# Two of eight experts: gates from one exponential of the second maximum, shares made on GpSimd, the last two halvings on VectorE, fewer filler matmuls

## The chip, the core and the metric

The kernel runs on one core of a Trainium2 chip. The metric is the device time of one execution in microseconds (us), median over runs; lower is better. Engine names in rows: PE is TensorE (matmuls), PEld its weight loads, DVE VectorE, ACT ScalarE, POOL GpSimd, SP SyncE. Everything is fp32, and on PE each matmul of the source shows as two instructions.

## What is computed

Four blocks follow one another on x (8 x 32 x 16 x 16), each a spatial mixer and a channel mixer with residuals. The channel mixer of the first and of the third block is the part that the change touches, a mixture of two experts out of eight for each of 2048 tokens:

```python
def _L0_ffn_ref(x, router_w, router_b, expert_w, expert_b):
    router_probs = jax.nn.softmax(x @ router_w + router_b, axis=-1)
    top_p, top_i = jax.lax.top_k(router_probs, K)            # K = 2 of E = 8
    top_p = top_p / jnp.sum(top_p, axis=-1, keepdims=True)
    expert_out = jnp.einsum('bnd,edc->bnec', x, expert_w) + expert_b
    gathered = jnp.take_along_axis(expert_out, top_i[..., None], axis=2)
    return jnp.einsum('bnk,bnkc->bnc', top_p, gathered)
```

With the maximum subtracted, the best logit is 0 and the second is d <= 0. The two shares are then 1 / (1 + exp(d)) and exp(d) / (1 + exp(d)).

## The kernel before

It is a hand-ordered program: each engine has one function with its instructions in program order, and engines wait for one another on named semaphores. Nothing is scheduled by a tool. The mixture of experts stands in each engine's `top2(turn)`; turn 0 lies at about 33.9 to 47.9 us of the profiled execution, turn 1 at 337.7 to 351.7 us. Tokens lie as 128 partitions x 16 tiles, so the logits LG, the masks S1 and S2, and the gates GW are 128 x 128 (16 tiles x 8 experts); a value per token is 128 x 16.

- VectorE (L762 to L779) makes the gates in a chain of sixteen small instructions, nearly each waiting for the one before. It takes the maximum (L762), subtracts it (L763, LG), finds the first maximum's place with ties broken by the tile `keys` (L765 to L767, S1), masks it (L768), takes the second maximum (L769) and finds its place in the same way (L770 to L773, S2), adds both masks (L774), multiplies by the exponentials EX of all logits (L776), sums (L777), inverts (L778) and scales (L779, GW).
- VectorE then multiplies the eight slots s of expert outputs by their gates (L788, 128 x 512 each, into PR); slots 0 to 3 come from SBUF (EXB), slots 4 to 7 from PSUM banks.
- GpSimd halves the products: L387 adds, for each of slots 0 to 6, the last four experts to the first four (semaphore `halved`). VectorE does slot 7 (L793, `last_halved`).
- ScalarE copies slot outputs 0 to 3 out of PSUM (L471, `keep(s)`, semaphore `expert_kept`) and, between `keep(0)` and `keep(1)`, makes EX from all logits (L475, waits `gate_ready`, which L763 gives).
- TensorE computes experts for slots 0 to 3, adds the residual (L1105), computes experts for slots 4 to 7 in banks that `keep` has emptied (L1203; its slot 4 + k waits for `expert_kept` of slot k), runs `keep_warm(FILL_GATES)`, transposes the gates (L1216), adds the expert biases (L1219), and then sums four experts of two slots into the output, four times (L1228, `pair` 0 to 3, eight instructions each). Ahead of each pair stand `FILL_PAIR` = 2 filler matmuls (L1101, results unused, two instructions each). Pair p waits for halving 2p + 2, pair 3 for halving 7 and `last_halved`. After pairs 1 and 3 `mixed_done` releases the sums of the next norm on VectorE (L708).

Of the kernel before, what the change touches and what calls it, by code (L numbers as in the profile page):

```python
# [18 lines left out]
E8 = 8  # L19
# [27 lines left out]
FILL_LAST = 1  # L47
FILL_TAIL = 16
FILL_KEYS = (0, 3)
FILL_GATES, FILL_PAIR = 4, 2  # L50
FILL, FILL_EC = (13, 18, 12, 6, 5, 9, 12, 8), 2
FILL_HOP, FILL_PROB, FILL_DRAIN = 2, 8, 3
GROUPS3 = 8
# [70 lines left out]
def metaformer(nc, x_in, cst_in, wa_in, wb_in, wc_in, wd_in, out):  # L124
# [3 lines left out]
    with ExitStack() as ctx:  # L128
# [7 lines left out]
        def view(t, col, dims, p0=0, n=P):  # L136

            if isinstance(t, tuple):
                t, first = t
                col = first + col  # L140
            if isinstance(t, Bank):
                t, col = psum, t.at + col
            w = t.shape[1]
            return bass.AP(t, p0 * w + col, [[w, n]] + [list(d) for d in dims])
# [77 lines left out]
        def cv(name, n, c=0, p0=0, np_=P):  # L222
# [23 lines left out]
            sem(n) for n in ("att_ready", "att_turned", "attc_ready", "u_done"))  # L246
        routed, gate_ready, ex_ready, expert_done, expert_kept, weighed = (
            sem(n) for n in ("routed", "gate_ready", "ex_ready", "expert_done", "expert_kept", "weighed"))
        halved, last_halved, mixed_done = sem("halved"), sem("last_halved"), sem("mixed_done")
        pa_set, h_turned, ht_ready = sem("pa_set"), sem("h_turned"), sem("ht_ready")  # L250
        gw_ready, gw_turned, gwt_ready = (sem(n) for n in ("gw_ready", "gw_turned", "gwt_ready"))
# [81 lines left out]
        def _(pool):  # L333
# [47 lines left out]

            def top2(turn):

                for s in range(NT // 2 - 1):
                    pool.wait_ge(weighed, turn * 8 + s + 1)
                    first, last = (view(PR, s * 512 + o, [[256, 2], [1, 128]]) for o in (0, 128))
                    pool.tensor_tensor(first, first, last, ALU.add).then_inc(halved, 1)  # L387
# [27 lines left out]
        def _(act):  # L415
# [52 lines left out]
            def top2(turn):  # L468
                def keep(s):
                    act.wait_ge(expert_done, turn * 8 + s + 1)  # L470
                    act.activation(view(EXB, s * 512, [[1, 512]]), bank[2 + s][:, :], ACT.Copy).then_inc(expert_kept, 1)  # L471

                keep(0)
                act.wait_ge(gate_ready, turn + 1)
                act.activation(EX[:, :], LG[:, :], ACT.Exp).then_inc(ex_ready, 1)  # L475
                for s in range(1, B4):
                    keep(s)
                act.wait_ge(gw_turned, turn + 1)
                act.activation(GT[:, 0:P], bank[1][:, 0:P], ACT.Copy).then_inc(gwt_ready, 1)
# [203 lines left out]
        def _(dve):  # L683
            links = [0]

            def link(ins):

                links[0] += 1
                ins.then_inc(dve_chain, 1)
                dve.wait_ge(dve_chain, links[0])  # L690
# [64 lines left out]
            def top2(turn):  # L755
# [10 lines left out]
                link(dve.tensor_reduce(s16[:, :], by_e(KEY), AX.X, ALU.max))  # L766
                link(dve.tensor_tensor(by_e(S1), by_e(KEY), one(s16), ALU.is_equal))  # L767
                link(dve.scalar_tensor_tensor(by_e(KEY), by_e(S1), -BIG, by_e(LG), ALU.mult, ALU.add))  # L768
                link(dve.tensor_reduce(s16[:, :], by_e(KEY), AX.X, ALU.max))  # L769
                link(dve.tensor_tensor(by_e(S2), by_e(KEY), one(s16), ALU.is_equal))  # L770
                link(dve.tensor_tensor(by_e(KEY), by_e(S2), keys, ALU.mult))
                link(dve.tensor_reduce(s16[:, :], by_e(KEY), AX.X, ALU.max))
                link(dve.tensor_tensor(by_e(S2), by_e(KEY), one(s16), ALU.is_equal))  # L773
                link(dve.tensor_tensor(by_e(S1), by_e(S1), by_e(S2), ALU.add))  # L774
                dve.wait_ge(ex_ready, turn + 1)
                link(dve.tensor_tensor(by_e(GW), by_e(S1), by_e(EX), ALU.mult))  # L776
                link(dve.tensor_reduce(s16[:, :], by_e(GW), AX.X, ALU.add))  # L777
                link(dve.reciprocal(mean[:, :], s16[:, :]))  # L778
                dve.tensor_tensor(by_e(GW), by_e(GW), one(mean), ALU.mult).then_inc(gw_ready, 1)  # L779
                dve.wait_ge(gw_ready, turn + 1)  # L780
                for s in range(NT // 2):
                    if s < B4:
# [2 lines left out]
                    else:  # L785
# [2 lines left out]
                    dve.tensor_tensor(view(PR, s * 512, [[256, 2], [C, E8], [1, C]]), outputs,  # L788
                                      view(GW, (s // 4 * 8 + s % 4) * E8, [[4 * E8, 2], [1, E8], [0, C]]),
                                      ALU.mult).then_inc(weighed, 1)  # L790
                dve.wait_ge(weighed, turn * 8 + 8)
                first, last = (view(PR, 7 * 512 + o, [[256, 2], [1, 128]]) for o in (0, 128))
                dve.tensor_tensor(first, first, last, ALU.add).then_inc(last_halved, 1)  # L793

            def expert_choice(turn, w, at):
                dve.wait_ge(ec_logits, turn + 1)
# [295 lines left out]
        def _(pe):  # L1092
# [93 lines left out]
            def top2(turn, w, at, nx):  # L1186
# [32 lines left out]
                    pe.matmul(moe_out[bh][0][:, 0:NPIX], GT[:, 0:P], w_(w, at["eb"] + bh * NPIX, NPIX), start=False, stop=False,  # L1219
                              skip_group_check=True)  # L1220
                for pair in range(4):
                    keep_warm(bank[0], FILL_PAIR)
                    bh, at_col = pair // 2, pair % 2 * 2 * C
                    pe.wait_ge(halved, turn * 7 + min(2 * pair + 2, 7))
                    if pair == 3:
                        pe.wait_ge(last_halved, turn + 1)
                    for e in range(E8 // 2):
                        ins = pe.matmul(view(moe_out[bh][0], at_col, [[P, 2], [C, 2], [1, C]]), ident,  # L1228
                                        view(PR, pair * 1024 + e * C, [[256, 2], [512, 2], [1, C]]), start=False,
                                        stop=(e == E8 // 2 - 1), skip_group_check=True)  # L1230
                    if pair % 2:
                        ins.then_inc(mixed_done, 1)
# [541 lines left out]
```

## Time and profile before

| | |
|---|---|
| median of three runs | 430.16 us (429.26 to 431.37) |
| the profiled execution: its own time, its span | 431.09 us, 429.3 us |
| PE busy (matmuls, ends modelled) | 385.1 us, 90% |
| DVE / ACT / POOL busy | 337.2 / 289.7 / 167.0 us |
| mean granted TensorE clock | 0.980 of full |
| L387 POOL | 14 instructions, 12.5 us |

A busy share says little here: in each stage another engine ends last. The time from the first to the last instruction (span) is 1.8 us less than the execution's own time. The views below are read at turn 1; turn 0 repeats them.

### The profile page before, as it was taken

The numbers are of one execution on the slowest core, as the hardware profiler recorded it, in microseconds if no ns is written. First come the engines' busy times: TensorE is split into PE (matmuls) and PEld (weight loads), VectorE is DVE, ScalarE is ACT, GpSimd is POOL, SyncE is SP. The second block draws the span as 40 slices with busy tenths as digits, with TensorE's granted clock in tenths as the row PEclk, the third lists the DMA queues.
The fourth block names the chain that finished last, engine by engine and source line by source line (L and its number), as shares of the span: only waits on it lengthen the run. The fifth ranks groups of instructions, "written<-read, shape, count | busy, mean of one in ns | idle before, by whom it ended". The sixth has DMA issues, their size and how long they took to land.

```text
span 429.3 us, 9890 instructions
## 1 busy us (share of the span) xinstructions
PE 385.1 (90%) x4018; PEld 261.6 (61%) x4018; DVE 337.2 (79%) x659; ACT 289.7 (67%) x513; POOL 167.0 (39%) x138
## 2 busy tenths in 40 slices
PE   5689999899899978989999888899999998898897
PEld 5467932223247746767678566667679686555575
DVE  3779697999971685999997677999996776999541
ACT  4755296998936486997751668987821537989471
POOL 4002300000000167799996466999993050000000
PEclk9898999999999998999999989999999899999999
DMA  8300040000024000000000000000000000000000
GB/s 294 129 3 2 2 94 2 2 2 0 2 94 175 2 2 2 2 2 2 2 2 0 2 2 2 2 2 2 2 2 2 0 2 1 2 2 2 2 2 26
DMA packets 1629, 9.29 MB, mean 22 GB/s; under 512 B 208, under 2 KB 976, under 8 KB 1104
## 3 DMA queue, kind: packets, MB, share of 16 engines
q1 hardware_dynamic: 1440, 8.59, 5.7%
q8 instruction: 32, 0.52, 0.5%
q14 instruction: 13, 0.11, 0.1%
q10 hardware_dynamic: 144, 0.07, 0.1%
HBM read 7.40 MB, written 0.26 MB: 18 GB/s over the span
## 4 chain that ended last, share of the span: by engine, by line
PE 40%; DVE 26%; ACT 16%; POOL 11%; issue 6%; DMA 1%; DVEq 0%; SPq 0%; ACTq 0%; POOLq 0%
PE bank L1431 7%; PE bank L1101 6%; PE bank L1353 4%; ACT RINGS L654 4%; POOL wb L371 4%; DVE RINGS L859 3%; DVE RINGS L850 3%; PE bank L1414 3%; PE bank L1575 2%; ACT RINGS L582 2%; PE bank L1555 2%; POOL RINGS L387 2%; POOL PRD L371 2%; PE bank L1342 2%; DVE PRD L953 2%
## 5 line engine op out<-in xcount | busy, mean ns | idle before, releaser
L1431 PE MATMUL bank<-VB,RINGS 64*128 64x144 f32 x1152 | 96.3, 304 | 8.9 <-DVE PRD L953 4.7
L1431 PEld LDWEIGHTS bank<-VB,RINGS 64*128 64x128 f32 x1152 | 77.7, 190 | 32.4 <-issue 15.3
L1101 PE MATMUL bank<-cst 128*128 128x128 f32 x450 | 63.1, 284 | 0.0
L1101 PEld LDWEIGHTS bank<-cst 128*128 128x128 f32 x450 | 56.3, 195 | 5.1 <-issue 2.7
L582 ACT ACTIVATE RINGS<-bank,cst 128x768 f32<-128x768 f32 x48 | 42.5, 886 | 22.1 <-PE bank L1414 22.1
L354 POOL TENSOR_TENSOR HY<-OM,cst 128x324 f32<-128x324 f32 x16 | 12.6, 816 | 113.0 <-DVE LXA L906 113.0
L953 DVE TENSOR_TENSOR wb<-bank,HY 128x864 f32<-128x864 f32 x48 | 50.4, 1049 | 5.4 <-PE bank L1431 5.4
L953 DVE TENSOR_TENSOR PRD<-bank,HY 128x864 f32<-128x864 f32 x48 | 50.2, 1050 | 5.5 <-PE bank L1431 5.5
L585 ACT ACTIVATE RINGS<-RINGS,cst 128x768 f32<-128x768 f32 x48 | 44.9, 936 | 1.6
L523 ACT ACTIVATE RINGS<-PRD,wb 128x2048 f32<-128x2048 f32 (+1 forms) x21 | 39.5, 1920 | 4.5 <-PE bank L1353 3.5
L1353 PE MATMUL bank<-RINGS,cst 128*32 128x512 f32 x336 | 39.7, 594 | 2.4 <-DVE RINGS L859 2.0
L1414 PE MATMUL bank<-RINGS,cst 32*128 32x256 f32 x288 | 35.0, 436 | 5.4 <-ACT RINGS L582 5.3
L371 POOL TENSOR_TENSOR wb<-wb 128x864 f32<-128x864 f32 x16 | 32.5, 2039 | 9.6 <-DVE wb L953 9.6
L371 POOL TENSOR_TENSOR PRD<-PRD 128x864 f32<-128x864 f32 x16 | 32.5, 2031 | 7.9 <-DVE PRD L953 7.9
L387 POOL TENSOR_TENSOR RINGS<-RINGS 128x256 f32<-128x256 f32 x14 | 12.5, 930 | 52.0 <-DVE RINGS L788 52.0
L654 ACT ACTIVATE RINGS<-RINGS,nm 128x256 f32<-128x256 f32 x64 | 31.5, 496 | 1.3 <-DVE nm L1056 1.3
L1353 PEld LDWEIGHTS bank<-RINGS,cst 128*32 128x32 f32 x336 | 10.3, 110 | 28.6 <-issue 18.2
L427 ACT ACTIVATE SQ<-XN 128x256 f32<-128x256 f32 x16 | 6.0, 417 | 31.2 <-DVE XN L713 31.2
L1575 PE MATMUL bank<-cst,RINGS 128*128 128x128 f32 x128 | 20.8, 286 | 4.9 <-ACT RINGS L654 4.4
L1056 DVE CUSTOM_DVE_ANT_0 RINGS<-bank,wd 128x256 f32<-128x256 f32 x64 | 22.7, 421 | 2.8 <-PE bank L1555 2.8
L380 POOL TENSOR_TENSOR PRD<-PRD 128x432 f32<-128x432 f32 (+1 forms) x16 | 24.8, 1575 | 0.0
L1414 PEld LDWEIGHTS bank<-RINGS,cst 32*128 32x128 f32 x288 | 15.5, 188 | 14.0 <-issue 9.5
(277 smaller groups left out, 713.8 us busy)
## 6 DMA issues: line engine op xcount, KB each, us to landing
wd<-in_wd SPq DMA_DIRECT2D x1, 2793.0 KB, 9.9
wb<-in_wb SPq DMA_DIRECT2D x1, 2112.0 KB, 10.3
wc<-in_wc SPq DMA_DIRECT2D x1, 1027.0 KB, 12.3
cst<-in_cst SPq DMA_DIRECT2D x1, 766.0 KB, 5.7
PRD<-PRD SPq DMA_DIRECT2D x1, 324.0 KB, 3.4
PRD<-PRD SPq DMA_DIRECT2D x1, 323.9 KB, 4.7
PRD<-PRD SPq DMA_DIRECT2D x1, 323.8 KB, 5.5
XC<-in_x SPq DMA_DIRECT2D x2, 128.0 KB, 2.4
```

The costliest lines, as they stand in the source:

```text
L371: pool.tensor_tensor(second, second, first, ALU.add).then_inc(paired, 1)
L380: pool.tensor_tensor(second, second, third, ALU.add).then_inc(paired, 1)
L523: return act.activation(out, x, ACT.Abs, scale=-1.0, bias=view(wb, WB["lw"] + 9 * g + tap, [[1, 1]]))
L582: act.activation(view(HX, hx, [[NPIX, 3], [1, NPIX]]), view(bank[4], 0, [[512, 3], [1, NPIX]]), ACT.Abs, bias=cv("mx", 1)).then_inc(abs_do ...
L585: act.activation(view(HX, hx, [[1, 3 * NPIX]]), view(HX, hx, [[1, 3 * NPIX]]), ACT.Relu, scale=-1.0, bias=cv("one", 1)).then_inc(hat_ready, 1)
L654: ins = act.activation(view(SM3, at, [[1, 256]]), view(SM3, at, [[1, 256]]), ACT.Exp, scale=-1.0, bias=nm[:, u:u + 1], accum_out=rs[:, u:u ...
L953: dve.tensor_tensor(view(prd(i, half), t * TRIO, [[3 * COLS, GP], [6 * NR, CG], [1, 6 * NR]]), view(bank[q % 2 * 2], 0, [[512, GP], [6 * N ...
L1101: pe.matmul(bk[:, 0:P], ident, ident, start=True, stop=True)
L1353: ins = pe.matmul(bank[2][32 * j:32 * j + 32, :], cv(rep, 32, 28 - 4 * g), two_images(slot, j), start=(n == 0), stop=(n == len(PE_JOBS) - ...
L1414: pe.matmul(bank[4 + quad][:, 0:NPIX], cv("select", P, t * P, 32 * quad, 32), view(LXT, i % 2 * NPIX, [[1, NPIX]], 32 * quad, 32), start=T ...
L1431: ins = pe.matmul(view(bank[q % 2 * 2 + gp], k3 * NR, [[3 * NR, 2 * CG], [1, NR]]), view(HX, b % 2 * HXN + (3 * t + k3) * NPIX + half * P, ...
L1575: ins = pe.transpose(turned3_bank[s % 3][:, (2 * kt + j) * P:(2 * kt + j + 1) * P], view(SM3, s % 6 * 512 + (2 * j + kt) * P, [[1, P]]), i ...
```

## The change

It makes the gates in another way, spreads them over three engines, moves one halving per turn, and leaves out three filler matmuls per turn. On VectorE the second maximum goes to `var` and is announced (`second_ready`). ScalarE no longer takes the exponential of all logits: it waits for `second_ready`, takes the exponential of the second maximum (128 x 16), waits for its own result, adds 1 to it (`Identity` with bias), and VectorE inverts the sum while it goes on finding the second mask. GpSimd multiplies the exponential by the inverse (tile `sd`) and the first mask by the inverse (S1). VectorE multiplies the second mask by `sd` and adds S1.

```diff
@@ -47,7 +47,7 @@
 FILL_LAST = 1
 FILL_TAIL = 16
 FILL_KEYS = (0, 3)
-FILL_GATES, FILL_PAIR = 4, 2
+FILL_GATES, FILL_PAIR, ON_POOL = 4, (2, 2, 1, 0), 6
 FILL, FILL_EC = (13, 18, 12, 6, 5, 9, 12, 8), 2
 FILL_HOP, FILL_PROB, FILL_DRAIN = 2, 8, 3
 GROUPS3 = 8
...
@@ -381,7 +382,11 @@
 
             def top2(turn):
 
-                for s in range(NT // 2 - 1):
+                by_e = view(S1, 0, [[E8, NT], [1, E8]])
+                pool.wait_ge(ratio_ready, turn + 1)
+                pool.tensor_tensor(sd[:, :], EX[:, 0:NT], mean[:, :], ALU.mult).then_inc(shares_ready, 1)
+                pool.tensor_tensor(by_e, by_e, view(mean, 0, [[1, NT], [0, E8]]), ALU.mult).then_inc(shares_ready, 1)
+                for s in range(ON_POOL):
                     pool.wait_ge(weighed, turn * 8 + s + 1)
                     first, last = (view(PR, s * 512 + o, [[256, 2], [1, 128]]) for o in (0, 128))
                     pool.tensor_tensor(first, first, last, ALU.add).then_inc(halved, 1)
@@ -471,8 +476,10 @@
                     act.activation(view(EXB, s * 512, [[1, 512]]), bank[2 + s][:, :], ACT.Copy).then_inc(expert_kept, 1)
 
                 keep(0)
-                act.wait_ge(gate_ready, turn + 1)
-                act.activation(EX[:, :], LG[:, :], ACT.Exp).then_inc(ex_ready, 1)
+                act.wait_ge(second_ready, turn + 1)
+                act.activation(EX[:, 0:NT], var[:, :], ACT.Exp).then_inc(ex_ready, 1)
+                act.wait_ge(ex_ready, 2 * turn + 1)
+                act.activation(EX[:, NT:2 * NT], EX[:, 0:NT], ACT.Identity, bias=cv("one", 1)).then_inc(ex_ready, 1)
                 for s in range(1, B4):
                     keep(s)
                 act.wait_ge(gw_turned, turn + 1)
@@ -766,17 +773,18 @@
                 link(dve.tensor_reduce(s16[:, :], by_e(KEY), AX.X, ALU.max))
                 link(dve.tensor_tensor(by_e(S1), by_e(KEY), one(s16), ALU.is_equal))
                 link(dve.scalar_tensor_tensor(by_e(KEY), by_e(S1), -BIG, by_e(LG), ALU.mult, ALU.add))
+                dve.tensor_reduce(var[:, :], by_e(KEY), AX.X, ALU.max).then_inc(second_ready, 1)
+                dve.wait_ge(second_ready, turn + 1)
+                link(dve.tensor_tensor(by_e(S2), by_e(KEY), one(var), ALU.is_equal))
+                link(dve.tensor_tensor(by_e(KEY), by_e(S2), keys, ALU.mult))
+                dve.wait_ge(ex_ready, 2 * turn + 2)
+                dve.reciprocal(mean[:, :], EX[:, NT:2 * NT]).then_inc(ratio_ready, 1)
                 link(dve.tensor_reduce(s16[:, :], by_e(KEY), AX.X, ALU.max))
                 link(dve.tensor_tensor(by_e(S2), by_e(KEY), one(s16), ALU.is_equal))
-                link(dve.tensor_tensor(by_e(KEY), by_e(S2), keys, ALU.mult))
-                link(dve.tensor_reduce(s16[:, :], by_e(KEY), AX.X, ALU.max))
-                link(dve.tensor_tensor(by_e(S2), by_e(KEY), one(s16), ALU.is_equal))
-                link(dve.tensor_tensor(by_e(S1), by_e(S1), by_e(S2), ALU.add))
-                dve.wait_ge(ex_ready, turn + 1)
-                link(dve.tensor_tensor(by_e(GW), by_e(S1), by_e(EX), ALU.mult))
-                link(dve.tensor_reduce(s16[:, :], by_e(GW), AX.X, ALU.add))
-                link(dve.reciprocal(mean[:, :], s16[:, :]))
-                dve.tensor_tensor(by_e(GW), by_e(GW), one(mean), ALU.mult).then_inc(gw_ready, 1)
+                dve.wait_ge(shares_ready, 2 * turn + 1)
+                link(dve.tensor_tensor(by_e(GW), by_e(S2), one(sd), ALU.mult))
+                dve.wait_ge(shares_ready, 2 * turn + 2)
+                dve.tensor_tensor(by_e(GW), by_e(GW), by_e(S1), ALU.add).then_inc(gw_ready, 1)
                 dve.wait_ge(gw_ready, turn + 1)
                 for s in range(NT // 2):
                     if s < B4:
@@ -788,9 +796,10 @@
                     dve.tensor_tensor(view(PR, s * 512, [[256, 2], [C, E8], [1, C]]), outputs,
                                       view(GW, (s // 4 * 8 + s % 4) * E8, [[4 * E8, 2], [1, E8], [0, C]]),
                                       ALU.mult).then_inc(weighed, 1)
-                dve.wait_ge(weighed, turn * 8 + 8)
-                first, last = (view(PR, 7 * 512 + o, [[256, 2], [1, 128]]) for o in (0, 128))
-                dve.tensor_tensor(first, first, last, ALU.add).then_inc(last_halved, 1)
+                for s in range(ON_POOL, NT // 2):
+                    dve.wait_ge(weighed, turn * 8 + s + 1)
+                    first, last = (view(PR, s * 512 + o, [[256, 2], [1, 128]]) for o in (0, 128))
+                    dve.tensor_tensor(first, first, last, ALU.add).then_inc(last_halved, 1)
 
             def expert_choice(turn, w, at):
                 dve.wait_ge(ec_logits, turn + 1)
@@ -1219,11 +1228,12 @@
                     pe.matmul(moe_out[bh][0][:, 0:NPIX], GT[:, 0:P], w_(w, at["eb"] + bh * NPIX, NPIX), start=False, stop=False,
                               skip_group_check=True)
                 for pair in range(4):
-                    keep_warm(bank[0], FILL_PAIR)
+                    keep_warm(bank[0], FILL_PAIR[pair])
                     bh, at_col = pair // 2, pair % 2 * 2 * C
-                    pe.wait_ge(halved, turn * 7 + min(2 * pair + 2, 7))
                     if pair == 3:
-                        pe.wait_ge(last_halved, turn + 1)
+                        pe.wait_ge(last_halved, 2 * (turn + 1))
+                    else:
+                        pe.wait_ge(halved, turn * ON_POOL + 2 * pair + 2)
                     for e in range(E8 // 2):
                         ins = pe.matmul(view(moe_out[bh][0], at_col, [[P, 2], [C, 2], [1, C]]), ident,
                                         view(PR, pair * 1024 + e * C, [[256, 2], [512, 2], [1, C]]), start=False,
```

The filler `FILL_GATES` stays 4. How this moves instructions is seen at three places. On VectorE, from the second maximum to the first multiplication of turn 0 (s, S and KEY are tiles of the gate chain), before:

```order
L769 TENSOR_REDUCE s<-KEY 128x16 [waits dve_chain]
L770 TENSOR_TENSOR S<-KEY,s 128x128 [waits dve_chain]
L771 TENSOR_TENSOR KEY<-S,cst 128x128 [waits dve_chain]
L772 TENSOR_REDUCE s<-KEY 128x16 [waits dve_chain]
L773 TENSOR_TENSOR S<-KEY,s 128x128 [waits dve_chain]
L774 TENSOR_TENSOR S<-S 128x128 [waits dve_chain]
L776 TENSOR_TENSOR GW<-S,EX 128x128 [waits ex_ready,dve_chain]
L777 TENSOR_REDUCE s<-GW 128x16 [waits dve_chain]
L778 RECIPROCAL mean<-s 128x16 [waits dve_chain]
L779 TENSOR_TENSOR GW<-GW,mean 128x128 [waits dve_chain]
L788 TENSOR_TENSOR RINGS<-RINGS,GW 128x512 [waits expert_kept,gw_ready]
```

and in the changed kernel (the mask is `S`, `sd` the second share, `var` the second maximum):

```order
L776 TENSOR_REDUCE var<-KEY 128x16 [waits dve_chain]
L778 TENSOR_TENSOR S<-KEY,var 128x128 [waits second_ready]
L779 TENSOR_TENSOR KEY<-S,cst 128x128 [waits dve_chain]
L781 RECIPROCAL mean<-EX 128x16 [waits ex_ready,dve_chain]
L782 TENSOR_REDUCE s<-KEY 128x16
L783 TENSOR_TENSOR S<-KEY,s 128x128 [waits dve_chain]
L785 TENSOR_TENSOR GW<-S,sd 128x128 [waits shares_ready,dve_chain]
L787 TENSOR_TENSOR GW<-GW,S 128x128 [waits shares_ready,dve_chain]
L796 TENSOR_TENSOR RINGS<-RINGS,GW 128x512 [waits expert_kept,gw_ready]
```

Nine instructions stood between the second maximum and the products; there are seven now, one of which (the reciprocal) the next doesn't wait for, and two waits on GpSimd (`shares_ready`) are new. On ScalarE, from the table load ahead of the stage, before:

```order
L420 ACT_TABLE_LOAD
L420 ACTIVATE spare<-cst 128x1
L471 ACTIVATE RINGS<-bank 128x512 [waits expert_done]
L475 ACTIVATE EX<-LG 128x128 [waits gate_ready]
L471 ACTIVATE RINGS<-bank 128x512 [waits expert_done] x3
L479 ACTIVATE GT<-bank 128x128 [waits gw_turned]
```

and in the changed kernel:

```order
L425 ACT_TABLE_LOAD
L425 ACTIVATE spare<-cst 128x1
L476 ACTIVATE RINGS<-bank 128x512 [waits expert_done]
L480 ACTIVATE EX<-var 128x16 [waits second_ready]
L482 ACTIVATE EX<-EX,cst 128x16 [waits ex_ready]
L476 ACTIVATE RINGS<-bank 128x512 [waits expert_done] x3
L486 ACTIVATE GT<-bank 128x128 [waits gw_turned]
```

One activation of 128 x 128 has become two of 128 x 16, the first of which waits for a later result of VectorE, the second for the first; three copies stand behind them. On TensorE, the four pairs of turn 0 and the filler between them (`bank<-cst` is filler, `bank<-RINGS,cst` a pair), before:

```order
L1101 MATMUL bank<-cst 128x128 x2
L1228 MATMUL bank<-RINGS,cst 128x2x64 [waits halved]
L1228 MATMUL bank<-RINGS,cst 128x2x64 x3
L1101 MATMUL bank<-cst 128x128 x2
L1228 MATMUL bank<-RINGS,cst 128x2x64 [waits halved]
L1228 MATMUL bank<-RINGS,cst 128x2x64 x3
L1101 MATMUL bank<-cst 128x128 x2
L1228 MATMUL bank<-RINGS,cst 128x2x64 [waits halved]
L1228 MATMUL bank<-RINGS,cst 128x2x64 x3
L1101 MATMUL bank<-cst 128x128 x2
L1228 MATMUL bank<-RINGS,cst 128x2x64 [waits last_halved,halved]
L1228 MATMUL bank<-RINGS,cst 128x2x64 x3
```

and in the changed kernel:

```order
L1110 MATMUL bank<-cst 128x128 x2
L1238 MATMUL bank<-RINGS,cst 128x2x64 [waits halved]
L1238 MATMUL bank<-RINGS,cst 128x2x64 x3
L1110 MATMUL bank<-cst 128x128 x2
L1238 MATMUL bank<-RINGS,cst 128x2x64 [waits halved]
L1238 MATMUL bank<-RINGS,cst 128x2x64 x3
L1110 MATMUL bank<-cst 128x128
L1238 MATMUL bank<-RINGS,cst 128x2x64 [waits halved]
L1238 MATMUL bank<-RINGS,cst 128x2x64 x3
L1238 MATMUL bank<-RINGS,cst 128x2x64 [waits last_halved]
L1238 MATMUL bank<-RINGS,cst 128x2x64 x3
```

The third pair has one filler matmul ahead of it and not two, the fourth none. GpSimd's list has two multiplications (128 x 16 and 128 x 128) ahead of the halvings, which are six and not seven; VectorE's has two halvings behind the products and not one.

## Rows read from the trace of the kernel before

**Rows 1.** Chain that ended last, turn 1: start us, us, what.

```profile
343.64 4.06 POOL RINGS L387 x4
347.75 1.16 PE bank L1228 x8
348.91 0.45 PE bank L1101 x4
...
351.66 0.42 DVE s L708
```

**Rows 2.** Same view, turn 0.

```profile
39.93 4.00 POOL RINGS L387 x4
...
47.89 0.42 DVE s L708
```

**Rows 3.** Timeline, turn 1, TensorE: start us, us, engine line op names shapes, idle before.

```profile
341.82 0.73 PEld L1203 LDWEIGHTS bank<-wc,XNC 32*128 32x128 f32 x10 [0.19 <-ACT RINGS L471]
...
343.87 0.27 PE L1216 MATMUL bank<-cst,GW 128*128 128x128 f32 x1
...
345.93 1.16 PE L1228 MATMUL bank<-RINGS,cst 128*128 128x128 f32 x8
...
346.93 0.61 PE L1101 MATMUL bank<-cst 128*128 128x128 f32 x4
...
350.57 1.06 PE L1228 MATMUL bank<-RINGS,cst 128*128 128x128 f32 x8
```

**Rows 4.** Timeline, turn 1, VectorE's gate chain.

```profile
339.66 0.29 DVE L769 TENSOR_REDUCE s<-KEY 128x16 f32<-128x128 f32 x1
...
339.99 0.29 DVE L770 TENSOR_TENSOR S<-KEY,s 128x128 f32<-128x128 f32 x1
...
342.26 0.25 DVE L778 RECIPROCAL mean<-s 128x16 f32<-128x16 f32 x1
...
342.87 3.56 DVE L788 TENSOR_TENSOR RINGS<-RINGS,GW 128x512 f32<-128x512 f32 x4
```

**Rows 5.** Timeline, turn 1, ScalarE.

```profile
339.51 0.60 ACT L471 ACTIVATE RINGS<-bank 128x512 f32<-128x512 f32 x1 [1.39 <-PE bank L1203]
...
340.00 0.30 ACT L475 ACTIVATE EX<-LG 128x128 f32<-128x128 f32 x1
340.20 1.56 ACT L471 ACTIVATE RINGS<-bank 128x512 f32<-128x512 f32 x3
```

**Rows 6.** One line each of ScalarE: ns min/median/max, first and last start.

```profile
L464 ACT ACTIVATE e<-den x1: 208/208/208, 25.1 to 25.1; 128x16 f32<-128x16 f32 x1
...
L431 ACT ACTIVATE sd<-var,cst x16: 300/301/303, 6.8 to 411.8; 128x8 f32<-128x8 f32 x16
```

**Rows 7.** Timeline in narrow windows, turn 1, single GpSimd halvings.

```profile
344.71 1.17 POOL L387 TENSOR_TENSOR RINGS<-RINGS 128x256 f32<-128x256 f32 x1
...
348.34 0.73 POOL L387 TENSOR_TENSOR RINGS<-RINGS 128x256 f32<-128x256 f32 x1
```

**Rows 8.** The same for VectorE's products and its halving.

```profile
342.87 0.69 DVE L788 TENSOR_TENSOR RINGS<-RINGS,GW 128x512 f32<-128x512 f32 x1
...
344.08 1.21 DVE L788 TENSOR_TENSOR RINGS<-RINGS,GW 128x512 f32<-128x512 f32 x1
...
348.86 0.49 DVE L793 TENSOR_TENSOR RINGS<-RINGS 128x256 f32<-128x256 f32 x1
```

**Rows 9.** GpSimd's groups by shape: busy us, mean ns, idle before.

```profile
L354 POOL TENSOR_TENSOR HY<-OM,cst 128x324 f32<-128x324 f32 x16 | 12.6, 816 | 113.0 <-DVE LXA L906 113.0
...
L1768 POOL MEMSET const-uint8-127<- 128x1 uint8 x1 | 0.1, 112 | 0.0
```

**Rows 10.** Windows: length, busy us of each engine, granted clock, DMA share, GB/s.

```profile
334.30:337.70 3.40, 2.50 (x19) 1.83 (x22) 1.29 (x5) 2.81 (x7) 0.00 (x0) 1.00 0.00 0
337.70:341.10 3.40, 3.40 (x20) 2.15 (x20) 3.04 (x11) 2.00 (x6) 0.00 (x0) 0.50 0.00 0
...
347.90:351.60 3.70, 3.70 (x34) 3.70 (x35) 1.75 (x4) 0.00 (x0) 2.03 (x3) 1.00 0.02 4
```

More of the change, by code:

```diff
@@ L248, in metaformer @@
             sem(n) for n in ("routed", "gate_ready", "ex_ready", "expert_done", "expert_kept", "weighed"))
+        second_ready, ratio_ready, shares_ready = sem("second_ready"), sem("ratio_ready"), sem("shares_ready")
         halved, last_halved, mixed_done = sem("halved"), sem("last_halved"), sem("mixed_done")
```

## The prediction, made before the changed kernel ran

> **What bounds the stage now.** I read the chain that ended last first, at the two places where the mixture of experts runs. The reader is to see that VectorE's gate chain leads into its first product, that then GpSimd's halvings carry the chain for 4.06 us, up to halving 4, and that from 347.75 us on TensorE carries it alone: pair 1, filler, pair 2, filler, pair 3, until VectorE's sum for the next norm starts at 351.66 us [rows 1]. Turn 0 reads the same, 8.0 us from GpSimd's start to that sum in both [rows 1, 2]. Whatever a turn gains at this sum is passed on to all that follows, since the next norm, and through it everything later, waits for it.
>
> Next I read TensorE's own timeline, to see what it could do if the products came earlier. Its gate transposition runs at 343.87 us, 1.0 us after the gates are ready (VectorE's first product starts at 342.87 us) [rows 3, 4]. So the gates are not what it waits for there: it is behind with slots 4 to 7, whose last part starts at 341.82 us, released by ScalarE's third copy after `keep(0)`, which ends at 340.20 + 1.56 = 341.76 us [rows 3, 5]. Behind it stand the filler of the gates, the transposition, the biases, and pair 0 at 345.93 us. Filler of four instructions follows at 346.93 us; at 0.45 us for four [rows 1] pair 1 could start at 347.37 us. It starts at 347.75, when halving 4 arrives. Waiting for GpSimd thus costs 0.38 us of the stage, and the rest of it is TensorE's own queue.
>
> **Fewer fillers.** One filler matmul goes ahead of pair 2 and two ahead of pair 3, six instructions of 0.45 / 4 = 0.1125 us [rows 1]: 0.67 us per turn, on the path, if the products are there in time. Those left out write a bank that nobody reads.
>
> **ScalarE.** `keep(1)` to `keep(3)` stand behind the exponential. Before, it started at 340.00 us, the copies at 340.20 us [rows 5]. Now it waits for the second maximum, which ends at 339.66 + 0.29 = 339.95 us [rows 4]. That costs almost nothing in this trace: `keep(0)` holds the engine until then in any case. The exponential is as that of L464, 128 x 16 in 0.21 us. The addition with a bias per partition is not in the trace at this size; from below it is 0.21 us (L464, no bias), from above 0.30 us (L431, 128 x 8 with scale and bias) [rows 6]. I take 0.30, since L431 too takes its bias from a tile. The copies overlap their predecessor by 0.10 us (0.30 long, 0.20 apart) [rows 5]. So the exponential runs 340.00 to 340.21, the addition from 340.24 to 340.54, the copies from 340.44: 0.24 us late, 0.15 with the lower bound. The last part of TensorE's slots is late by the same 0.24 us, and with it the whole queue up to pair 0. This is the price of the change.
>
> On what the addition costs, the Trainium skill (ScalarE: Activation LUTs, What ACT_TABLE_LOAD costs) gives an activation 186 ns plus 0.833 ns a column, and some 93 ns more for each operand per partition. An estimate from that page is 0.20 and 0.29 us for the two, against the rows' 0.21 and 0.30; by it the delay would be 0.23 us, and the same page's figure of a table load does not arise, since the order shows no load between the two functions.
>
> **VectorE.** Instructions of the chain follow at 0.33 us (339.66 to 339.99) [rows 4]. The second mask's first two start at 339.99 and 340.31; the reciprocal at 340.64, just behind the sum from ScalarE (340.54). Its 0.25 us [rows 4] is not waited for by the next instruction, which starts at about 340.81, allowing 0.08 us of overlap; then 341.14, 341.46, 341.79, and the first product at 342.11. That is 0.76 us earlier than 342.87. I call this advance s.
>
> **GpSimd.** It answers VectorE in 0.08 us (product ends at 342.87 + 0.69 = 343.56, halving starts at 343.64) [rows 1, 8]. Its share instructions are not in the trace. The nearest rows are a fill of one column, 0.11 us, and L354, 324 columns in 0.82 us [rows 9]; between them lies the halving, 256 columns in 0.73 us [rows 7]. On that line 16 columns take 0.15 us and 128 columns 0.42 us; the bounds are 0.11 and 0.82 for each. They would run from 340.97 to 341.12 and from 341.09 to 341.51, in time for the instructions at 341.46 and 341.79.
>
> But the two engines get in each other's way. Halvings take 1.17 us while VectorE multiplies from SBUF, 0.73 us alone, and a product then takes 1.21 us against 0.69 [rows 7, 8]. Each waits for about one whole instruction of the other. The second share would start just ahead of VectorE's mask instruction (341.14), which reads two tiles of SBUF, and hold it until 341.51. After such a hold the product in the rows finished 0.55 us later, 0.14 less than alone (first halving 343.64 to 344.74, the product ends at 344.08 + 1.21 = 345.29) [rows 8], so the mask ends at 341.51 + 0.29 - 0.14 = 341.66 rather than 341.43: s = 0.76 - 0.23 = 0.53 us. The Trainium skill (SBUF — State Buffer, Who interferes with whom) has the rule: a VectorE instruction with two SBUF inputs and a GpSimd one that reads SBUF exclude one another for a whole instruction, and the one issued first wins. The trace agrees (1.17 against 0.73 us). By the rule s is 0.53, without it 0.76; it speaks against putting shares on GpSimd beside this chain, and it doesn't change the sum below, for which 0.40 is enough.
>
> **The halvings.** All of GpSimd's and VectorE's work on products moves s earlier. Halving 6 ends at 348.34 + 0.73 = 349.07 before [rows 7], 348.54 now. VectorE now does two at the end in place of one; at 0.49 us [rows 8] less 0.08 overlap that adds 0.41, so both are done at 348.86 + 0.49 + 0.41 - 0.53 = 349.23. GpSimd's halving 7 no longer exists.
>
> **The sum, turn 1.** TensorE's queue gives pair 0 at 345.93 + 0.24, pair 1 at 347.37 + 0.24 = 347.61 (halving 4 was at 347.75, less 0.53 is 347.22: in time), pair 2 after 0.90 and 0.225 of filler at 348.74 (halving 6 at 348.54: in time by 0.2 less some 0.06 of response), pair 3 at 349.64 (halved at 349.23), and its end 1.06 us later [rows 3] at 350.70. Before it was 350.57 + 1.06 = 351.63. Gain 0.93 us: 0.67 filler, 0.38 of waiting that vanishes, less 0.24 on ScalarE, and 0.12 because a pair that has been stopped starts up slowly (from pair 1 to pair 3 it was 350.57 - 347.75 = 2.82 us, and two pairs and two fillers at 0.1125 an instruction are 2.70). Turn 0 has the same intervals, so 1.9 us in all. The profiled execution would go from 431.09 us to 429.2 (span 429.3 to 427.4), and its 431.09 lies 0.9 above the median of the runs, 430.16; the prediction for the median is 430.16 - 1.9 = **428.3 us**, 0.44% less.
>
> **Rivals.**
>
> *ScalarE's delay is hidden or small* (chance 0.16). If the addition takes 0.21 and the copies had slack, the gain is up to 1.17 a turn, 427.8 us. For it: the lower bound of the addition. Against: L431's 0.30 us [rows 6], and the row of 341.82, which names ScalarE as releaser [rows 3].
>
> *The products come too late for pair 2* (0.16). Pair 2 starts at 349.07 + 0.06 - s or when TensorE is free; then 0.90 and 1.06: end 351.09 - s. It decides below s = 0.40. If GpSimd's shares cost 0.6 us more than I take, s is about 0, the gain 0.54 a turn, 429.1 us.
>
> *The shares come very late, and the kernel gets slower* (0.07). One mechanism: VectorE's last two gate instructions wait for `shares_ready`, all products wait behind them, and GpSimd starts a form that no row has, with an operand repeated eight times. From s = -0.54 on the kernel loses, 2 us per us. If the second share took 2.0 us in place of 0.42, s would be -1.05 and the stage would end at 352.14, 0.5 later per turn: 431.2 us. Against it: GpSimd's L354 has a repeated operand too, and costs 0.82 us.
>
> *Too little filler* (0.09). After a stretch in which TensorE was busy for 2.50 of 3.40 us, the next stretch of 3.4 us was granted 0.50, the lower level of 1.2 GHz; pairs run at 1.00, or 2.4 GHz [rows 10]. Work on TensorE in such a stretch takes twice as long, up to 1.7 us lost. One more such stretch gives 430.0 us, two 431.7. Against it: the fillers go where TensorE has work queued at once, so its busy share doesn't fall. The Trainium skill (TensorE: Matmul & The Clock Gate, What's actually happening) says that recent activity decides the clock, and by it leaving out filler is a risk only where idling takes its place.
>
> *The change does nothing measurable* (0.05): stretches at the lower clock fall otherwise and eat the gain, 430.2 us.
>
> **Numbers.** The forecast has 0.47, within 0.5 us of 428.3. Two executions of the same kernel differ by up to 2.1 us (429.26 to 431.37), so some 0.5% is what a measurement can tell from no change: below 428.0 is faster, above 432.3 slower. About four tenths of the forecast, nearly all of the first rival and a little of the rest lie below 428.0: faster 0.37. Slower by over 0.5% needs two stretches more at the lower clock and lost products, or shares later by over 2 us: 0.07. The rest, 0.56, is the same. The range for 8 in 10 is 427.0 to 429.7: the first rival with its lower bound, up to the second with a little less than its full loss of s.
>
> **What would show it.** Right: the second instruction of ScalarE lasts about 0.3 us and its copies start 0.24 us later after the second maximum than before; no idle time of TensorE on GpSimd ahead of pairs 1 and 2; the first product starts 0.5 us or more earlier after the second maximum; from the first maximum to the next norm's second sum some 0.93 us less. Wrong: TensorE waits for GpSimd or VectorE between pairs, the reciprocal waits for ScalarE, share instructions of over 0.8 us, or a changed number of stretches at the lower clock, which would move the total by up to 1.7 us with the stages unchanged.

## The result, and the profile after

The changed kernel took 434.48 us (median of 5 runs, 434.08 to 438.61) against 430.5 us before (5 runs); the ratio is 1.011 with an interval of 1.006 to 1.016. In a later set of runs (e7 below) it took 434.03 us (12 runs, 429.05 to 434.89) against 431.14, ratio 1.005 (1.0015 to 1.008). The ratios are taken over the executions and are not quotients of the medians (434.48 / 430.5 would be 1.009), and they leave out an execution over 1.5% above the fastest of its kernel (two of e2's). It is slower, where 428.3 us with a range up to 429.7 was forecast. Its times fall in groups: 12 of these 17 executions took 434.0 us or more, three took 429.1. So the median, which lies in the upper group, moved more than the mean: in the later set the means are 432.7 and 430.9 us. Of the kernel before none took over 433 us.

I call **stage** what lies between the start of the first maximum and the start of the second sum of the next norm on VectorE: 47.89 - 33.93 = 13.96 us in turn 0 before, 351.66 - 337.71 = 13.95 in turn 1 [rows 1, 2]. The first maxima of the profile before are these rows of its timeline:

```profile
33.93 0.29 DVE L762 TENSOR_REDUCE s<-bank 128x16 f32<-128x128 f32 x1
...
337.71 0.29 DVE L762 TENSOR_REDUCE s<-bank 128x16 f32<-128x128 f32 x1 [2.02 <-PE bank L1192]
```

In the profiled execution after (434.08 us, span 432.2) it is 15.82 us in turn 0 and 14.29 in turn 1. The span grew by 2.9 us: 1.85 and 0.34 in the stages, 0.89 ahead of the first stage, where no instruction was altered, -0.20 between the stages, 0.01 behind. The chain that ended last, turn 0 after (start us, us, what):

```profile
37.09 0.22 ACT EX L480
37.31 0.03 issue
37.34 0.31 ACT EX L482
37.65 0.49 ACT RINGS L476
38.14 0.04 issue
38.18 3.05 PE bank L1212 x14
41.23 2.01 PE bank L1110 x8
...
43.81 2.07 PE bank L1228 x4
```

In place of 4 us of GpSimd [rows 1, 2] the chain runs over ScalarE's two activations, the copy behind them, and then over TensorE's own queue: slots, filler, biases. GpSimd's halvings are no longer in it. The timeline of TensorE and ScalarE there shows why the queue is long:

```profile
35.80 0.60 ACT L476 ACTIVATE RINGS<-bank 128x512 f32<-128x512 f32 x1 [0.58 <-PE bank L1212]
...
36.78 0.69 PE L1212 MATMUL bank<-wb,XNC 32*128 32x256 f32 x2
...
37.09 0.22 ACT L480 ACTIVATE EX<-var 128x16 f32<-128x16 f32 x1 [0.69 <-DVE var L776]
...
37.34 0.31 ACT L482 ACTIVATE EX<-EX,cst 128x16 f32<-128x16 f32 x1
...
37.55 1.55 ACT L476 ACTIVATE RINGS<-bank 128x512 f32<-128x512 f32 x3
...
38.18 3.05 PE L1212 MATMUL bank<-wb,XNC 32*128 32x256 f32 x14 [0.71 <-ACT RINGS L476]
...
41.16 2.08 PE L1110 MATMUL bank<-cst 128*128 128x128 f32 x8
...
43.81 2.07 PE L1228 MATMUL bank<-wb,GT 128*128 128x256 f32 x4 [0.37 <-ACT GT L486]
```

ScalarE's first copy starts 0.98 us after the first maximum (34.82), not 1.8 us after it as in the profile before (339.51 - 337.71). Its exponential then waits 0.69 us for the second maximum, the copies with it, and TensorE waits 0.71 us for a copy. After that eight filler instructions take 2.08 us, which take 1.16 us at the higher clock (e5, below). The windows say at what clock (length; busy us, with counts, of TensorE, its weight loads, VectorE, ScalarE and GpSimd; granted clock as a share of 2.4 GHz; DMA share and GB/s):

```profile
35.50:39.00 3.50, 2.79 (x18) 1.55 (x10) 3.15 (x12) 2.48 (x6) 0.63 (x2) 1.00 0.00 0
39.00:42.40 3.40, 3.40 (x18) 2.50 (x17) 3.37 (x5) 0.10 (x1) 2.34 (x3) 0.50 0.00 0
42.40:45.80 3.40, 3.03 (x10) 2.27 (x10) 3.40 (x7) 1.76 (x3) 3.08 (x4) 0.50 0.00 0
```

TensorE was busy for 2.79 of 3.50 us at 2.4 GHz, and for the next 6.8 us it was granted 1.2 GHz, over slots 4 to 7, the gates' filler, the transposition and the biases. Before, the 1.2 GHz lay over the first 3.4 us of the stage [rows 10], where TensorE has slack.

### The profile page after: what moved, and what is told of

Its sections match the earlier page's. It is cut to its first block, busy times and chain, and to the rows that moved or that the text cites. A ratio compares the mean times of both kernels' runs of the same rounds, so it can differ in the third digit from the quotient of the medians.

```text
span 432.2 us, 9870 instructions
## 1 busy us (share of the span) xinstructions
PE 387.0 (90%) x4006; PEld 263.6 (61%) x4006; DVE 336.8 (78%) x657; ACT 290.4 (67%) x515; POOL 166.6 (39%) x140
## 4 chain that ended last, share of the span: by engine, by line
PE 46%; DVE 22%; ACT 16%; POOL 9%; issue 6%; DMA 1%; DVEq 0%; SPq 0%; ACTq 0%
PE bank L1110 7%; PE bank L1441 7%; PE bank L1363 6%; ACT RINGS L661 4%; POOL wb L372 4%; PE bank L1424 2%; PE bank L1585 2%; DVE RINGS L868 2%; DVE RINGS L859 2%; ACT RINGS L589 2%; PE bank L1565 2%; POOL PRD L372 2%; PE bank L1352 2%; DVE PRD L962 2%; PE bank L1238 2%
## 5 line engine op out<-in xcount | busy, mean ns | idle before, releaser
L364 POOL TENSOR_TENSOR HY<-HY,OM 128x324 f32<-128x324 f32 x32 | 23.6, 761 | 0.9 <-ACT HY L581 0.9
```

## The experiments

All ratios are to the kernel before, run on the same chip. e1 to e4 ran on one chip, e5 to e8 and then e9 to e11 on another, each of the three sets beside its own runs of the kernel before. The expectations weigh three causes. Theory W: ScalarE's copies wait, TensorE idles for them and is then granted 1.2 GHz. Rival F: too little filler. Rival G: GpSimd's shares or the moved halving.

**e1, the wait alone.** The kernel before, its exponential still over all logits:

```diff
-                act.wait_ge(gate_ready, turn + 1)
+                act.wait_ge(second_ready, turn + 1)
                 act.activation(EX[:, :], LG[:, :], ACT.Exp).then_inc(ex_ready, 1)
...
-                link(dve.tensor_reduce(s16[:, :], by_e(KEY), AX.X, ALU.max))
+                dve.tensor_reduce(s16[:, :], by_e(KEY), AX.X, ALU.max).then_inc(second_ready, 1)
+                dve.wait_ge(second_ready, turn + 1)
```

> The kernel before, with one thing of the change alone: ScalarE's exponential of all logits waits for the second maximum, and so do the three copies behind it. Theory W (the copies stand behind a later result, TensorE idles for them, and is then granted 1.2 GHz while it works through slots 4 to 7, filler and biases): most of the loss appears, +2 to +5 us against before, and the profile has a stretch at 0.50 inside the stage after the copies. Rival F (too little filler is the cause): no change, within 0.5 us, since all fillers are here. Rival G (GpSimd's shares or the moved halving): no change either.

Measured: 432.6 us (12 runs), ratio 1.0045 (1.002 to 1.007). Three of 12 executions took 435.9 to 436.8 us, beyond anything of the kernel before. Its profile holds both cases. Turn 1 has the 1.2 GHz at its start, and the stage takes 13.94 us, the same as in the kernel before: there the wait costs nothing. Turn 0 does not, and takes 16.34 us. Timeline and windows of turn 0:

```profile
37.36 0.31 ACT L476 ACTIVATE EX<-LG 128x128 f32<-128x128 f32 x1 [0.69 <-DVE s L770]
...
38.21 2.94 PE L1205 MATMUL bank<-wb,XNC 32*128 32x256 f32 x14 [0.47 <-ACT RINGS L472]
```

```profile
35.90:39.30 3.40, 2.93 (x18) 1.67 (x15) 3.04 (x11) 2.37 (x5) 0.00 (x0) 1.00 0.00 0
39.40:42.70 3.30, 3.30 (x17) 2.50 (x14) 3.20 (x7) 0.00 (x0) 1.61 (x2) 0.50 0.00 0
```

The same wait of 0.69 us and the same 1.2 GHz behind it, with all fillers in place and with neither shares on GpSimd nor a moved halving. The median moved by less than theory W said (1.4 us, not 2 to 5): one part of the change gives this loss in some executions only.

**e2, the fillers back.** The changed kernel with `FILL_PAIR` (2, 2, 2, 2) in place of (2, 2, 1, 0).

> The changed kernel with two filler matmuls ahead of every pair again. Theory W: the stretch at 1.2 GHz begins ahead of the pairs and so stays; the fillers lie on TensorE's path and cost up to 0.67 us a turn, 435 to 436 us. Rival F: the loss goes, 429 to 431 us. Rival G: 434 to 435 us.

Measured: 434.04 us (12 runs, 430.59 to 438.1), ratio 1.005 (1.002 to 1.008). The loss stays; the means of all executions would give 1.007. Turn 0 took 16.58 us with 1.2 GHz from 4.5 to 11.4 us of the stage, turn 1 13.62 with it at the start. Rival F falls. The median is not the 435 to 436 us of theory W; it lies where rival G had it, so e2 does not tell W from G. e1 has the loss without G's parts, and e5 below is without the loss with all of them.

**e4, the fillers alone.** The kernel before with (2, 2, 1, 0).

> The kernel before with the fillers of the change alone (2, 2, 1, 0). Theory W: pair 1 still waits for halving 4, after it up to 0.67 us a turn less on TensorE, but halvings 6 and 7 (349.07 and 349.93 us) then hold the pairs; 0.3 to 0.6 us a turn gained, 429 to 430 us. Rival F: slower than before by 2 us or more. Rival G: as theory W.

Measured: 431.83 us (12 runs), ratio 1.000 (0.998 to 1.002), where 429 to 430 us were expected. Both stages took 13.50 us, 0.45 less than before as expected, with no 1.2 GHz in them. But the whole is no faster: the profile has a stretch of 3.4 us at 1.2 GHz at 370.7 us, where the others have none, and 78.57 us behind the second stage in place of 77.64. Leaving out filler does not slow the stage; whether it draws that later stretch, one profile can't say.

**e3 and e9, one more copy ahead of the wait.** The changed kernel with ScalarE's order altered:

```diff
                 keep(0)
+                keep(1)
                 act.wait_ge(second_ready, turn + 1)
...
-                for s in range(1, B4):
+                for s in range(2, B4):
                     keep(s)
```

> The changed kernel, but ScalarE makes two copies and not one before it waits for the second maximum. Theory W: the second copy no longer waits, TensorE gets slot 5 some 1.2 us earlier, the third and fourth copies about 0.5 us earlier, its idle time in the stage shrinks by about as much, and the time falls by 1 to 4 us, to 430 to 433 us. Rival F and rival G: no change beyond 0.5 us (the exponential itself comes at the same moment).

Measured: 428.26 us (6 runs, 427.74 to 429.46), ratio 0.993 (0.990 to 0.995), below the 430 to 433 us expected. I ran it again, on the other chip:

> The changed kernel with two copies ahead of the wait for the second maximum, once more, since its ratio of 0.993 came from few runs. Theory W: 428 to 430 us, ratio 0.992 to 0.998, no executions at 434 us or above, and with full clock at the stage's start the third copy starts about 2.75 us and the fourth 3.25 us after the first maximum's start. If its first result was luck of the clock, it scatters like the changed kernel, up to 434 us.

Measured: 428.98 us (12 runs), ratio 0.998 (0.9955 to 1.000). One of 18 executions took over 430.5 us (433.78). The stage took 13.05 and 13.58 us in e3's profile, 12.90 and 12.78 in e9's. ScalarE in e3, turn 0:

```profile
36.07 1.08 ACT L476 ACTIVATE RINGS<-bank 128x512 f32<-128x512 f32 x2 [1.13 <-PE bank L1213]
...
37.04 0.22 ACT L481 ACTIVATE EX<-var 128x16 f32<-128x16 f32 x1
...
37.29 0.31 ACT L483 ACTIVATE EX<-EX,cst 128x16 f32<-128x16 f32 x1
37.50 1.06 ACT L476 ACTIVATE RINGS<-bank 128x512 f32<-128x512 f32 x2
```

The second copy fills the wait, and none is left there. In e9's turn 1, at 2.4 GHz throughout, 0.20 us of it is left and TensorE waits 0.55 us for a copy, where it waits 0.71 us in the changed kernel; its third and fourth copies start 2.74 and 3.21 us after the first maximum, as expected. This order beats the changed kernel clearly; how far it beats the kernel before, 0.7% (6 executions) or 0.2% (12), the two sets leave open.

**e5, fillers where TensorE idled.** The changed kernel with one line more on TensorE, ahead of slots 4 to 7:

```diff
+                keep_warm(bank[0], 5)
                 experts(1)
                 keep_warm(bank[0], FILL_GATES)
```

> The changed kernel, with five filler matmuls between the residual and slots 4 to 7, where TensorE idled for ScalarE's copies. Nothing on ScalarE, VectorE or GpSimd is altered. If it is the granted clock that costs (idling ahead of the biases and pairs, then 1.2 GHz), the stage is granted 2.4 GHz after its copies more often, and the time falls by 1 to 3 us to 431 to 433 us, though no instruction that is needed comes earlier. If it is only the late copies (a plain wait), the time stays at 434 to 435 us or rises by what the fillers take, up to 1.1 us a turn.

**e7, the changed kernel again**, on the same chip.

> The changed kernel once more, for further times and another profile of it beside the others of this call. Theory W: where a profile has its 1.2 GHz stretch at the stage's first instruction, as the kernel before had, the stage takes 13.0 to 13.1 us, as predicted; where it has it later, over slots 4 to 7 and the biases, 14 us and more. If the loss lies in the instructions themselves, the stage takes over 14 us in either case.

Measured: e5 428.96 us (12 runs, 427.69 to 432.82), ratio 0.9975 (0.995 to 1.000), below the 431 to 433 us expected; e7 434.03 us (12 runs). Ten instructions more per turn, in idle time, take 5 us off the median and 3.1 us off the mean (432.7 to 429.6 us). Turn 1 of e5, timeline and windows:

```profile
337.73 1.28 PE L1110 MATMUL bank<-cst 128*128 128x128 f32 x10
...
338.13 0.21 ACT L480 ACTIVATE EX<-var 128x16 f32<-128x16 f32 x1 [0.68 <-DVE var L776]
...
338.94 2.39 PE L1212 MATMUL bank<-wc,XNC 32*128 32x256 f32 x16
...
341.26 1.16 PE L1110 MATMUL bank<-cst 128*128 128x128 f32 x8
```

```profile
335.90:339.30 3.40, 3.40 (x33) 2.82 (x29) 3.05 (x12) 2.09 (x7) 0.18 (x1) 1.00 0.00 0
339.30:342.70 3.40, 3.23 (x25) 2.22 (x23) 3.30 (x7) 0.99 (x3) 2.12 (x4) 1.00 0.00 0
```

ScalarE waits 0.68 us as before and its copies come no sooner, yet TensorE stays at 2.4 GHz, the eight filler instructions take 1.16 us again and the stage 12.88 us. So it is the clock that costs, not the late copies. GpSimd's shares and the moved halving are all in e5, and so rival G falls too.

e7's profile holds the other half of the proof. In its turn 1 the stretch at 1.2 GHz covers the start of the stage, as in the profile from which I predicted:

```profile
339.29 0.29 DVE L769 TENSOR_REDUCE s<-bank 128x16 f32<-128x128 f32 x1 [2.04 <-PE bank L1201]
...
343.87 3.56 DVE L796 TENSOR_TENSOR RINGS<-RINGS,GW 128x512 f32<-128x512 f32 x4
...
352.33 0.42 DVE L715 TENSOR_REDUCE s<-bank 128x8 f32<-128x256 f32 x1 [1.30 <-PE bank L1238]
```

```profile
339.00:342.40 3.40, 3.40 (x21) 2.35 (x21) 2.65 (x10) 1.81 (x6) 0.00 (x0) 0.50 0.00 0
```

352.33 - 339.29 = 13.04 us; the prediction's sum was 13.95 - 0.93 = 13.02. Its turn 0, with 1.2 GHz from 5.1 to 11.9 us of the stage, took 15.89. The same instructions, 2.85 us apart.

**e6, the kernel before again.**

> The kernel before once more, for another profile. Its stage took 13.95 us with the 1.2 GHz stretch at its start. Theory W: with a stretch elsewhere or none it takes 13.9 to 14.0 us all the same unless the stretch lies over the pairs, since halving 4 holds pair 1 back and TensorE has slack until then. If it is 13.5 or less without a stretch, then the clock costs the kernel before as well.

Measured: 431.16 us (8 runs), ratio 1.001 (0.999 to 1.003). Turn 0 has no 1.2 GHz and takes 13.94 us, turn 1 has it at the start and takes 13.94 too. Turn 0:

```profile
36.56 0.60 ACT L471 ACTIVATE RINGS<-bank 128x512 f32<-128x512 f32 x1 [0.58 <-PE bank L1203]
...
37.06 0.30 ACT L475 ACTIVATE EX<-LG 128x128 f32<-128x128 f32 x1
...
37.26 1.56 ACT L471 ACTIVATE RINGS<-bank 128x512 f32<-128x512 f32 x3
...
43.79 1.16 PE L1228 MATMUL bank<-RINGS,cst 128*128 128x128 f32 x8 [0.65 <-POOL RINGS L387]
...
45.61 1.16 PE L1228 MATMUL bank<-RINGS,cst 128*128 128x128 f32 x8 [0.21 <-POOL RINGS L387]
```

At 2.4 GHz the exponential does not wait, the last three copies start 1.68 us after the first maximum (35.58), and TensorE is early, so that it waits 0.65 us for GpSimd ahead of pair 0. The kernel before is indifferent to the clock at the start of its stage, because GpSimd ends the wait in either case.

**e11, the wait with fillers.** e1 with e5's line.

> The kernel before with the exponential that waits for the second maximum (432.6 us, ratio 1.0045), and five fillers ahead of slots 4 to 7. If the granted clock after idling is the whole price of that wait, the executions at 436 us vanish and the time is that of the kernel before or up to 1 us less, 430 to 431 us, since halving 4 still holds pair 1. If the wait costs by itself, 432 to 433 us.

Measured: 430.53 us (12 runs, 429.29 to 432.7), ratio 1.000 (0.998 to 1.002). No execution is at 436 us; both stages take 13.94 and 13.95 us without 1.2 GHz. The wait, with its idling filled, costs nothing.

**e8 and e10, more of it.** e8 is e3 with three filler matmuls (six instructions) ahead of slots 4 to 7; e10 is e5 with `FILL_GATES` 1 and not 4.

> Two copies ahead of the wait for the second maximum, which gave 428.3 us, and three filler matmuls ahead of slots 4 to 7. If idling there still draws a 1.2 GHz stretch in some executions, the time falls by up to 1 us more, to 427.3 us; if it no longer does, the fillers delay slots 4 to 7 by at most 0.67 us a turn and the time is 428.3 to 429.5 us.

> The changed kernel with five fillers ahead of slots 4 to 7 and one in place of four behind them, ahead of the gates' transposition. Theory W: idling is filled where it arises, and TensorE's path behind the last copy is shorter by three fillers, 0.67 us a turn at 2.4 GHz, of which the arrival of halving 6 leaves about 0.3; 0.5 to 1 us less than the same kernel with four behind (428.96 us), 428 to 428.5 us. If fillers behind the slots are what keeps the clock up, the time rises to 430 us and more.

Measured: e8 429.23 us (12 runs, 427.21 to 432.59), ratio 0.997 (0.994 to 1.000); e10 429.59 us (12 runs), ratio 0.997 (0.995 to 0.9996). Neither is told from e9 or e5; three of e8's executions still took 432.3 to 432.6 us. The windows of e8's turn 1, whose stage starts at 336.10 us, show a limit of both remedies:

```profile
335.20:338.60 3.40, 3.40 (x23) 2.45 (x23) 2.26 (x8) 1.53 (x4) 0.00 (x0) 0.50 0.00 0
338.60:341.90 3.30, 3.30 (x18) 2.73 (x20) 2.46 (x9) 1.91 (x6) 0.66 (x2) 0.50 0.00 0
```

TensorE does not idle, but comes into the stage at 1.2 GHz and keeps it for 5.9 us. The stage takes 14.04 us, 0.1 more than the kernel before and 0.46 more than e3's turn 1 under the same stretch (13.58): there the fillers are themselves on the path. e10 missed what was expected: its stages took 12.83 and 12.78 us, 0.1 less than e5's 12.88 and not 0.3, and its median is not lower. The versions that come out ahead (e5, e8, e9, e10) gain 0.2 to 0.3%, with intervals that end at or near 1; only e3 shows more.

| profile | turn 0: 1.2 GHz in the stage, us from its start | stage us | turn 1: the same | stage us |
|---|---|---|---|---|
| before | 0 to 3.4 | 13.96 | 0 to 3.4 | 13.95 |
| e6, before again | none | 13.94 | 0 to 3.3 | 13.94 |
| after | 4.2 to 11.0 | 15.82 | 5.9 to 9.3 | 14.29 |
| e7, after again | 5.1 to 11.9 | 15.89 | 0 to 3.1 | 13.04 |
| e1, the wait alone | 4.2 to 11.1 | 16.34 | 0 to 3.4 | 13.94 |
| e2, fillers back | 4.5 to 11.4 | 16.58 | 0 to 3.3 | 13.62 |
| e4, the fillers alone | none | 13.50 | none | 13.50 |
| e3, one more copy first | 0.3 to 3.7 | 13.05 | 0 to 5.6 | 13.58 |
| e9, e3 again | 0.4 to 3.8 | 12.90 | none | 12.78 |
| e8, e3 with fillers | 0.3 to 3.7 | 13.04 | 0 to 5.9 | 14.04 |
| e5, fillers in the wait | 0 to 3.4 | 13.28 | none | 12.88 |
| e10, e5 with fewer behind | none | 12.83 | none | 12.78 |
| e11, the wait with fillers | none | 13.94 | none | 13.95 |

A stretch that began up to 1.2 us ahead of the stage is written from 0. The table holds 26 stages. Twelve have 1.2 GHz at or within 0.4 us of their start, and none of these has another stretch. The other fourteen start at 2.4 GHz. In five of them ScalarE waits 0.69 us for the second maximum and nothing fills TensorE's idle time (after, both turns; turn 0 of e7, e1 and e2), and all five are granted 1.2 GHz from 4 to 6 us on. In nine there is no such wait, or fillers or the second copy take its place, in e9 all but 0.20 us of it (e6's turn 0; e4, e10 and e11, both turns; turn 1 of e5 and e9), and none of them is granted 1.2 GHz at all.

## Why the prediction was wrong

**The step that failed** stands under ScalarE: "That costs almost nothing in this trace: `keep(0)` holds the engine until then in any case." It was true of the trace and not of the kernel. `keep(0)` ended just at the second maximum only because that profile had TensorE at 1.2 GHz over the first 3.4 us of both stages, which made slot 0 late: the copy started 1.80 us after the first maximum. At 2.4 GHz it starts at 0.99 us (e6, e7 turn 0, after), the exponential then waits 0.69 us, and the second copy starts 2.73 us after the first maximum in place of 1.68 us, 1.05 us late and not 0.24. I had the rows for it, 0.50 in the very window from which I took the start of `keep(0)` [rows 10], and did not ask what the other clock would do.

**What took its place** is not the 0.8 us by which this exceeds the predicted delay, but what they draw. TensorE idles for them, is granted 1.2 GHz next, and now every instruction up to the pairs lies on the path. Filling the idle time takes the median down by 5 us (e5 against e7), and the wait alone, without the other edits, gives a stage of 16.34 us (e1). The Trainium skill (TensorE: Matmul & The Clock Gate, What's actually happening) says that how busy TensorE has been recently decides the clock. The rows agree: busy for 2.79 of 3.50 us, then 1.2 GHz (after); busy for 3.40 of 3.40 us, then 2.4 GHz (e5). I had cited that rule and found no idling, because I looked for it between the pairs.

**Fewer fillers**: 0.67 us a turn on the path. Right in e7's turn 1, where the sum came out at 13.04 us. That it came so near is in part luck: `keep(0)` started 0.13 us later than the prediction had it, and pair 1 followed pair 0 0.09 us sooner (1.35 us behind it, against 1.44). In the kernel before, alone, the fewer fillers gave 0.45 (e4), as halving 6 then holds pair 2. The rival "too little filler" had about the right price, up to 1.7 us for each stretch of 3.4 us (e7's turn 0, with 6.8 us, took 2.85 us more than its turn 1), and the wrong cause; putting them back did not help (e2).

**ScalarE's addition**: 0.31 us, taken 0.30. With `keep(0)` at the same moment (1.93 us after the first maximum), the second copy starts at 2.88 us in e7 and 2.62 in e6, 0.26 later; predicted 0.24. The estimate beside it, given as 0.23 us, adds up to 0.22 (0.20 + 0.03 + 0.29 - 0.10, less 0.20 before); nothing hangs on it.

**GpSimd's shares and VectorE**: 0.22 and 0.45 us, taken 0.15 and 0.42. Both engines in the profile after, turn 0:

```profile
38.15 0.22 POOL L387 TENSOR_TENSOR sd<-EX,mean 128x16 f32<-128x16 f32 x1 [32.22 <-DVE mean L781]
38.18 0.34 DVE L783 TENSOR_TENSOR S<-KEY,s 128x128 f32<-128x128 f32 x1
...
38.33 0.45 POOL L388 TENSOR_TENSOR S<-S,mean 128x128 f32<-128x128 f32 x1
38.55 0.38 DVE L785 TENSOR_TENSOR GW<-S,sd 128x128 f32<-128x128 f32 x1
```

The first product starts 4.48 us after the first maximum in turn 0 after, 4.42 in turn 1, and 4.57 in e7's turn 1, 5.16 before: s is 0.68, 0.74 and 0.59 us, predicted 0.53. The hold that the prediction read from the halvings is there: VectorE's instruction ends 0.15 us after the share beside it (38.37 to 38.52 us, 38.78 to 38.93), as 0.29 less 0.14 had it. It costs less, since the second share starts 0.15 us behind the mask instruction and not ahead of it: the mask took 0.34 us and the next 0.38, against 0.29 alone, 0.14 us in all and not 0.23. In e7's turn 1 the reciprocal waits 0.18 us for ScalarE, which the prediction named as a sign of being wrong, and s is the smallest there.

**The total.** In its own case the prediction held; it gave that case a chance of 0.47 and gave none to the case that most executions have. The slower rival (shares late) was not what happened. The 0.89 us ahead of the first stage in the profile after is not the change's: the first maximum starts at 33.57 to 35.76 us over the thirteen profiles, 33.93 and 35.58 in the two of the kernel before, with the place of the first stretch at 1.2 GHz.

**What stays open.** Idle time elsewhere is not always followed by 1.2 GHz: e6's turn 0 has TensorE busy for 2.53 of 3.40 us (42.4 to 45.8 us) and stays at 2.4 GHz. Where the stretches fall differs between executions of one kernel, and I could neither set it nor read it for executions without a profile; that the group at 434 us has 1.2 GHz late in both stages rests on one profile (after; e7's execution, late in one stage only, took 431.85 us). The amount of 1.2 GHz does not make the groups: of e7's executions the three at 429.1 us had a mean granted clock of 0.976, and so had five of the seven at 434 us or more, which leaves the place of the stretches. The time between the two stages also moves, 288.2 to 291.3 us over the thirteen profiles, by where the stretches fall there, and the small differences between e3, e5, e8, e9 and e10 drown in that.

## What to carry to other kernels

A slack that a profile shows beside a stretch at the lower clock is a slack of that execution; before a wait is costed at nothing, work out when its cover would end at the other clock. Ahead of a short result that arrives late, put what is ready first on an in-order engine: one copy moved ahead of the exponential turned the loss into a small gain. Where TensorE must idle ahead of a queue that will be the path, fillers in the idle time are worth far more than fillers in the queue; where it comes in at the lower clock and does not idle, they cost (e8's turn 1).

## What was not expected of the hardware

Ten instructions whose results nobody reads, 1.28 us of TensorE per turn, took 5 us off the kernel's median (434.03 to 428.96 us) and 3.1 us off its mean. And a stretch of 1.2 GHz can protect: the stage of the changed kernel is fastest relative to before (13.04 against 13.94 us) when TensorE is slow in its first 3.4 us, and took up to 2.85 us more when it was fast there.
